# A graph convolution with a residual layer norm: VectorE multiplies both halves of a chunk's vector products in one operation and the selections of two chunks in one operation

## The chip, the cores and the metric

One Trainium2 chip, one of its cores. The time is device microseconds (us) of one execution of the whole program, and the number to predict is the median of a few executions. A few of the profile's times are in nanoseconds (ns) and say so.

## What is computed

12,500 nodes have 128 features each, 32 scalars and 32 vectors of three components. 412,500 edges, sorted by destination, carry four attributes (one scalar, one vector) and eight radial numbers. For each edge the features of its source are gathered, weighted by a small network of the radial numbers and by the attributes, and summed at the destination:

```
h = gelu(gelu(edge_scalar_attr @ W_mlp1) @ W_mlp2)
w00, w01, w10, w11 = h @ Wp_00, h @ Wp_01, h @ Wp_10, h @ Wp_11
out0_a = w00 * e0 * ea0
out0_b = w11 * sum(e1 * ea1, -1) / sqrt(3)
out1_a = (w01 * e0)[:, :, None] * ea1[:, None, :]
out1_b = w10[:, :, None] * e1 * ea0[:, :, None]
n0, n1 = segment_sum([out0_a, out0_b]), segment_sum([out1_a, out1_b])
x = layernorm(x + mix(self(x), n0 @ W2_0e, n1 @ W2_1o))
```

`e0` and `e1` are the scalar and vector features of the edge's source node. Everything is float32 apart from a few small helpers in bfloat16.

## The kernel before

The engines are named as in the profile: PE (TensorE), DVE (VectorE), ACT (ScalarE), POOL (GpSimd), SP (SyncE, which here issues loads and stores alone). They run written-out instruction streams of their own and meet at semaphores.

**Start and end.** The first 155 us transform the nodes, write a table of features to HBM and turn the indices round; the last 84 us finish the last edges, normalise the rows and store them. Between them stands the loop over the edges, which this study is about.

**Blocks, chunks, tiles.** The edges go in 202 blocks of 2048. A block has four chunks (0 to 3) of four tiles, a tile is 128 edges, one per partition. What one block needs, engine by engine:

- POOL gathers the source rows of each tile by an indirect DMA whose indices lie in SBUF (`gather`, L456): 16 a block, 4 a chunk. The gathered rows have four slots, so POOL may run up to four blocks ahead. Before the first gather of block b it waits until chunk 3 of block b-4-1 has been summed by PE and until the indices are there; before chunk c, until DVE has made the products of chunk c of block b-4, which frees the slot.
- PE and ACT make the radial weights (`radial`, L778, out of two layers with a gelu each: PE L764, ACT L551, PE L769, ACT L557). The two layers run several blocks ahead of their use, in halves: each half is a ping-pong of PE, ACT, PE, ACT through one PSUM bank.
- DVE makes for each chunk the products of weights (in PSUM) and gathered rows (in SBUF). `multiply` has one operation for the two scalar parts (L1042, 256 elements a partition) and two for the vector parts (L1045, 384 elements each, half h = 0 and half h = 1). DVE also compares destinations with a window of 32 nodes (`compare`, L1024, once a block) to a 0/1 mask `sel01`, multiplies the mask by the four attributes (`select`, L1032: one operation of 512 elements per chunk, called for two chunks at a time), and adds a finished window into the accumulator (L1073, four a block).
- PE sums the products into the window by matmuls with the selection as weights (`segment_sum`, L790, 32 recorded matmuls a block), transposes the sums (L798) and every fourth block applies the output weights (L805). ACT copies in between (L564 to L566, L570).

**The order on DVE.** One turn (`cycle`) for block b is: products of chunks 2 and 3 of block b, compare for block b+1, products of chunk 0, select for chunks 0 and 1, products of chunk 1, select for chunks 2 and 3, four window additions of an earlier block. Only the last select of a block signals PE (`s_sel`), and each chunk's last product signals for itself (`s_prod`). The products of chunk 2 wait for PE's sum of chunk 2 of the block before (`s_seg`).

**The order on PE.** In a turn it runs second layer, weights of chunk 2, first layer, weights of chunk 3, transposes, second layer, weights of chunks 0 and 1 of a later block, then the 32 matmuls of the segment sums, every fourth turn the output weights, and last a first layer. The body of the hardware loop is eight turns, the loop variable is in the addresses and wait values.

Of the kernel before, what the change touches and what calls it, by code (L numbers as in the profile page):

```python
# [10 lines left out]
ALU = mybir.AluOpType  # L11
# [5 lines left out]
MUL, RADIAL, HID = 32, 8, 64  # L17
# [19 lines left out]
CT = TILES // CHUNKS  # L37
# [7 lines left out]
WINDOW = 32  # L45
# [3 lines left out]
RING = 2 * SUPER  # L49
# [19 lines left out]
def build_program(nc, x, src, dst, ea4, ea8, W1_0e, W1_1o, W_mlp1, W_mlp2, Wp, W2_0e, W2_1o, out):  # L69
# [3 lines left out]
    with ctx:  # L73
        def sb(name, shape, dt=FP32):
            return ctx.enter_context(nc.sbuf_tensor(name, shape, dt))
# [15 lines left out]
        ea_t = sb("ea_t", [128, RING, TILES, 4])  # L91
# [5 lines left out]
        sel = sb("sel", [128, 2, TILES, 4, WINDOW])  # L97
# [44 lines left out]
        sel01 = big.bitcast(BF16)[:, 2 * 12288:2 * 12288 + TILES * WINDOW].rearrange("p (t w) -> p t w", t=TILES)  # L142
# [116 lines left out]
        def nodes_of(j):  # L259
            return 128 if j < NODE_J else REST  # L260
# [25 lines left out]
        for e in range(2):  # L286
            h = slice(HID * e, HID * (e + 1))
# [636 lines left out]
        def _(dve):  # L924
# [37 lines left out]
            for n in range(NODE_BATCHES):  # L962
# [5 lines left out]
                if n < NODE_BATCHES - 1:  # L968
                    last = dve.tensor_copy(feat_rows[:, piece % PIECE_SLOTS, j:j + BATCH, :],
                                           bank[2 + n % 2][:, :].rearrange("p (j f) -> p j f", j=BATCH))  # L970
                else:
                    for i, t in enumerate(batch_tiles(n)):
                        last = dve.tensor_copy(feat_rows[0:nodes_of(t), piece % PIECE_SLOTS, j + i, :],
                                               bank[2 + n % 2][0:nodes_of(t), 128 * i:128 * (i + 1)])
# [52 lines left out]

            def select(b, s, chunks):
                dve.wait_ge(s_sel0, b + 1)
                for c in chunks:  # L1030
                    t = slice(CT * c, CT * (c + 1))
                    last = dve.tensor_tensor(sel[:, s % 2, t], sel01[:, t, :].unsqueeze(2).to_broadcast([128, CT, 4, WINDOW]),  # L1032
                                             ea_t[:, s % RING, t, :].unsqueeze(3).to_broadcast([128, CT, 4, WINDOW]), ALU.mult)
                if CHUNKS - 1 in chunks:
                    last.then_inc(s_sel, 1)

            def multiply(weights, rows, to, n):

                w = weights.rearrange("q (t h a u) -> q t h a u", t=n, h=2, a=2)
                f = rows.rearrange("q t (s u) -> q t s u", s=4)  # L1040
                o = to.rearrange("q t (h s u) -> q t h s u", h=2, s=4)
                dve.tensor_tensor(o[:, :, :, 0, :], w[:, :, :, 0, :],  # L1042
                                  f[:, :, 0, :].unsqueeze(2).to_broadcast([128, n, 2, MUL]), ALU.mult)
                for h in range(2):
                    last = dve.tensor_tensor(o[:, :, h, 1:4, :],  # L1045
                                             w[:, :, h, 1, :].unsqueeze(2).to_broadcast([128, n, 3, MUL]),
                                             f[:, :, 1:4, :], ALU.mult)
                return last

            def products(b, s, c, round_):  # L1050
                dve.wait_ge(s_w[c], b + 1)
                dve.wait_ge(s_g[s % SLOTS][c], round_ * (16 * CT) + 16 * CT)
                if c < 2 and s > 1:
                    dve.wait_ge(s_seg[c], b - 1)
                if c >= 2 and s > 0:
                    dve.wait_ge(s_seg[c], b + 0)
                multiply(wgt_ps[c][:, :], gath[:, s % SLOTS, CT * c:CT * (c + 1), :], prod_at(s, c), CT).then_inc(s_prod[c], 1)
# [17 lines left out]
            def cycle(b, s, n, first_add=2, last=False):  # L1075
                if s >= 0:
                    products(b, s, 2, n * 2 + s // SLOTS)
                    products(b, s, 3, n * 2 + s // SLOTS)
                if s >= -1:
                    compare(b + 1, s + 1, (n + (s + 1) // RING) * 16 + 16)  # L1080
                    if not last:
                        products(b + 1, s + 1, 0, n * 2 + (s + 1) // SLOTS)
                    select(b + 1, s + 1, range(0, 2))
                    if not last:
                        products(b + 1, s + 1, 1, n * 2 + (s + 1) // SLOTS)
                    select(b + 1, s + 1, range(2, CHUNKS))
                    base = load_bases(b - 5) if s >= first_add else None
                if s >= first_add:
                    add_windows(b - 5, s - 5, n * (RING // CONV) + (s - 5) // CONV + 1, base)
# [27 lines left out]
            with dve.If(flag < WINDOW):  # L1117
# [8 lines left out]
                n = ROUNDS - 1  # L1126
# [78 lines left out]
```

## Time and profile before

| | |
|---|---|
| times of three executions | 5050.67, 5320.28, 5044.24 us |
| median | 5050.67 us |
| span of the profiled execution | 5064.0 us |
| busy in it: PE, POOL, DVE, ACT | 3676, 3174, 1878, 1336 us |
| granted TensorE clock, mean | 0.853 |

The profiled execution is one more run, 13.3 us over the median. Its page gives busy time and instructions of each engine, the costliest groups of instructions and the idle time ahead of them with what ended it. "remote" there means that the semaphore update that ended the wait could not be put down to an instruction's recorded end. The timeline has one row per instruction, or per run of like instructions: start and duration in us, engine, line, operation, tiles, count, and in brackets the idle time of the engine ahead of it. The tile names `big` and `dst_rows` stand for reused memory: as an output of L1042 and L1045 they are the products, as an output of L1024 and an input of L1032 the mask.

### The profile page before, as it was taken

The page shows a single profiled execution, that of the slowest core. Times are in us where ns is not written, and L with a number is a line of the kernel's source. Part 1 is how long each engine was busy: PE and PEld are TensorE (multiplying, and loading weights), DVE is VectorE, ACT ScalarE, POOL GpSimd, SP SyncE. Part 2 cuts the span into 40 slices and gives each one's busy share as a digit, 9 for nine tenths or more (in the row PEclk, how much of TensorE's full clock was granted, in tenths as well). Part 3 has the DMA queues.
Part 4 walks back from the last instruction along what each step waited for, and adds up shares of the span by engine and source line. Part 5 has one row for each costly group of instructions (what it writes and reads, how often), then busy time and mean ns, then how long its engine had stood idle before and what let it go on. Part 6 is the DMA issues. An engine that isn't in the chain of part 4 may idle for free.

```text
span 5064.0 us, 44347 instructions
## 1 busy us (share of the span) xinstructions
PE 3676.4 (73%) x13222; PEld 2593.1 (51%) x13222; DVE 1877.7 (37%) x4551; ACT 1336.2 (26%) x2651; POOL 3173.6 (63%) x3262
## 2 busy tenths in 40 slices
PE   7667777777777776667787777677677777777776
PEld 4445455545555544445555555455455545555555
DVE  4333333333334333333433333333333334333335
ACT  4222222222222222222222222222222222222224
POOL 5556666666666665556666666666666666666660
PEclk8788888888888887888888888888888888888887
DMA  4111211211211111111112111111111111111111
GB/s 160 46 43 48 50 46 48 50 46 48 50 47 48 50 46 44 41 44 47 47 48 50 46 48 50 46 48 50 46 46 48 49 47 47 50 48 46 48 45 57
DMA packets 244371, 254.65 MB, mean 50 GB/s; under 512 B 162332, under 2 KB 188703, under 8 KB 242800
## 3 DMA queue, kind: packets, MB, share of 16 engines
q0 software_dynamic: 103616, 211.52, 16.0%
q1 hardware_dynamic: 139024, 42.54, 3.4%
q10 hardware_dynamic: 1696, 0.18, 0.0%
q8 instruction: 15, 0.25, 0.0%
q14 instruction: 20, 0.16, 0.0%
HBM read 241.18 MB, written 12.80 MB: 50 GB/s over the span
## 4 chain that ended last, share of the span: by engine, by line
another core or an unknown queue 57%; PE 28%; ACT 8%; issue 6%; DVE 1%; ACTq 0%; DVEq 0%; POOL 0%; POOLq 0%
PE bank L778 9%; PE bank L769 9%; PE bank L764 6%; ACT h L551 3%; PE bank L790 2%; PE bank L798 1%; ACT big L557 1%; ACT idx L536 1%; ACT ztsb L570 1%; ACT big L622 1%; ACT dst_rows L566 1%; ACT dst_rows L565 1%; ACT dst_rows L564 0%; PE bank L710 0%
## 5 line engine op out<-in xcount | busy, mean ns | idle before, releaser
L456 POOL DMA_INDIRECT gath<-feature_table,idx x3224 | 3151.4, 977 | 1765.7 <-issue 1632.3
L769 PE MATMUL bank<-h,w2bd 128*128 128x512 f32 x800 | 590.7, 829 | 1249.3 <-ACT h L551 1154.6
L1042 DVE TENSOR_TENSOR big<-bank,gath 128x256 f32<-128x256 f32 x606 | 254.9, 421 | 2952.3 <-remote 2656.2
L551 ACT ACTIVATE h<-bank 128x512 f32<-128x512 f32 x400 | 238.9, 597 | 3320.3 <-remote 2863.0
L790 PE MATMUL bank<-big,sel 128*128 128x256 f32 x4848 | 1084.1, 380 | 11.2 <-DVE big L1045 7.3
L778 PEld LDWEIGHTS bank<-wpbd,big 128*128 128x128 f32 x3224 | 747.7, 232 | 524.3 <-issue 364.2
L790 PEld LDWEIGHTS bank<-big,sel 128*128 128x128 f32 x4848 | 924.2, 191 | 138.3 <-issue 7.5
L778 PE MATMUL bank<-wpbd,big 128*128 128x256 f32 x3224 | 971.1, 442 | 1.2 <-DVE big L1045 1.2
L769 PEld LDWEIGHTS bank<-h,w2bd 128*128 128x128 f32 x800 | 153.5, 240 | 1421.3 <-ACT h L551 1317.4
L1045 DVE TENSOR_TENSOR big<-bank,gath 128x384 f32<-128x384 f32 x1212 | 614.0, 549 | 0.0
L1032 DVE TENSOR_TENSOR sel<-big,ea_t 128x512 f32<-128x512 bf16 x808 | 527.9, 695 | 0.0
L557 ACT ACTIVATE big<-bank 128x512 f32<-128x512 f32 x400 | 437.6, 1094 | 93.3 <-PE bank L769 35.0
L790 PE MATMUL bank<-dst_rows,sel 128*128 128x256 f32 x1600 | 361.6, 379 | 0.0
L790 PEld LDWEIGHTS bank<-dst_rows,sel 128*128 128x128 f32 x1600 | 303.9, 190 | 41.3
L764 PE MATMUL bank<-e8T,w1bd 128*128 128x512 f32 x400 | 261.0, 738 | 28.2 <-ACT big L557 19.7
L764 PE MATMUL bank<-dst_rows,w1bd 128*128 128x512 f32 x400 | 256.3, 728 | 30.6 <-ACT big L557 29.2
L1045 DVE TENSOR_TENSOR dst_rows<-bank,gath 128x384 f32<-128x384 f32 x400 | 202.8, 550 | 0.0
L1073 DVE TENSOR_TENSOR acc<-acc,bank 128x32 f32 x806 | 149.8, 186 | 140.6 <-remote 39.1
L805 PE MATMUL bank<-ztsb,dst_rows 128*128 128x512 f32 (+1 forms) x408 | 183.4, 593 | 0.7 <-ACT ztsb L570 0.7
L570 ACT COPY ztsb<-bank 128x512 f32<-128x512 f32 x202 | 118.3, 586 | 180.8 <-PE bank L798 89.8
L564 ACT COPY dst_rows<-bank 32x256 f32<-32x256 f32 x403 | 142.6, 354 | 35.8 <-PE bank L790 31.0
L566 ACT COPY dst_rows<-bank 64x256 f32<-64x256 f32 x403 | 147.9, 367 | 4.8
(90 smaller groups left out, 1426.5 us busy)
## 6 DMA issues: line engine op xcount, KB each, us to landing
gath<-feature_table,idx POOLq DMA_INDIRECT x3224
e<-in_edge_attr SPq DMA_DIRECT2D x204, 64.0 KB
ea_t<-in_edge_attr SPq DMA_DIRECT2D x100, 64.0 KB
feature_table<-gath SPq DMA_DIRECT2D x4, 1280.0 KB, 5.7
out<-big SPq DMA_DIRECT2D x4, 1280.0 KB
big<-in_x SPq DMA_DIRECT2D x3, 1280.0 KB, 10.1
dst_rows<-in_dst SPq DMA_DIRECT2D x1, 1536.0 KB
big<-in_src SPq DMA_DIRECT2D x1, 1280.0 KB
```

The costliest lines, as they stand in the source:

```text
L456: pool.indirect_dma_start(out=gath[:, s % SLOTS, t, :], out_offset=None, in_=table[:, :], in_offset=bass.IndirectOffsetOnAxis(ap=idx[:, s, ...
L551: act.activation(h1[:, h, :], hid_ps[:, :], ACT.Gelu_apprx_tanh, scale=1.0 / math.sqrt(RADIAL)).then_inc(s_h1[h], 1)
L557: act.activation(h2_columns(k // SUPER % 2, 2 * m + h), hid_ps[:, :].rearrange("q (b c p) -> q b c p", b=SUPER, c=CHUNKS), ACT.Gelu_apprx_ ...
L566: act.copy(to[64:128], z_ps[pair][64:128, :, 128:256]).then_inc(s_zc, 1)
L764: pe.matmul(hid_ps[:, :], w1bd[:, 2 * (k % SUPER) + h, :], e8T[k // SUPER % 2][:, :], start=True, stop=True)\
L769: pe.matmul(hid_ps[:, :], w2bd[:, :], h1[:, h, :], start=True, stop=True).then_inc(s_h2p[h], 1)
L778: last = pe.matmul(wgt_ps[c][:, 256 * r:256 * (r + 1)], h2[:, s // SUPER % 2, s % SUPER, c, r, :, :].rearrange("q p l -> q (p l)"), wpbd[: ...
L790: last = pe.matmul(z_ps[c // 2][:, c % 2, :], sel[:, s % 2, CT * c + t, :, :].rearrange("q k w -> q (k w)"), prod_at(s, c)[:, t, :], start ...
L805: last = pe.matmul(y_ps[:, 0:128 * n], conv[:, k, :], ztsb[:, k, 0:n, :, :].rearrange("q b c w -> q (b c w)"), start=(k == 0), stop=(k == 3))
L1032: last = dve.tensor_tensor(sel[:, s % 2, t], sel01[:, t, :].unsqueeze(2).to_broadcast([128, CT, 4, WINDOW]), ea_t[:, s % RING, t, :].unsqu ...
L1042: dve.tensor_tensor(o[:, :, :, 0, :], w[:, :, :, 0, :], f[:, :, 0, :].unsqueeze(2).to_broadcast([128, n, 2, MUL]), ALU.mult)
L1045: last = dve.tensor_tensor(o[:, :, h, 1:4, :], w[:, :, h, 1, :].unsqueeze(2).to_broadcast([128, n, 3, MUL]), f[:, :, 1:4, :], ALU.mult)
```

## The change

Two helpers of DVE are written with wider access patterns. The loop over the halves in `multiply` goes: one operation with 768 elements a partition takes the place of two with 384. The loop over chunks in `select` goes: one operation with 1024 elements takes the place of two with 512. All waits and signals stay at the same places, and so do the orders of the other engines.

```
             def select(b, s, chunks):
                 dve.wait_ge(s_sel0, b + 1)
-                for c in chunks:
-                    t = slice(CT * c, CT * (c + 1))
-                    last = dve.tensor_tensor(sel[:, s % 2, t], sel01[:, t, :].unsqueeze(2).to_broadcast([128, CT, 4, WINDOW]),
-                                             ea_t[:, s % RING, t, :].unsqueeze(3).to_broadcast([128, CT, 4, WINDOW]), ALU.mult)
+                t, n = slice(CT * chunks[0], CT * (chunks[-1] + 1)), CT * len(chunks)
+                last = dve.tensor_tensor(sel[:, s % 2, t], sel01[:, t, :].unsqueeze(2).to_broadcast([128, n, 4, WINDOW]),
+                                         ea_t[:, s % RING, t, :].unsqueeze(3).to_broadcast([128, n, 4, WINDOW]), ALU.mult)
                 if CHUNKS - 1 in chunks:
                     last.then_inc(s_sel, 1)
...
                 dve.tensor_tensor(o[:, :, :, 0, :], w[:, :, :, 0, :],
                                   f[:, :, 0, :].unsqueeze(2).to_broadcast([128, n, 2, MUL]), ALU.mult)
-                for h in range(2):
-                    last = dve.tensor_tensor(o[:, :, h, 1:4, :],
-                                             w[:, :, h, 1, :].unsqueeze(2).to_broadcast([128, n, 3, MUL]),
-                                             f[:, :, 1:4, :], ALU.mult)
-                return last
+                return dve.tensor_tensor(o[:, :, :, 1:4, :],
+                                         w[:, :, :, 1, :].unsqueeze(3).to_broadcast([128, n, 2, 3, MUL]),
+                                         f[:, :, 1:4, :].unsqueeze(2).to_broadcast([128, n, 2, 3, MUL]), ALU.mult)
```

On DVE, the second turn of the opening (the turns written out ahead of the hardware loop) before the change, from the products of chunk 2 to the scalar product of chunk 1; in brackets stand the semaphores waited for, and `x2` is two instructions:

```order
L1042 TENSOR_TENSOR big<-bank,gath 128x8x32 [waits segments_summed2,gathered1_2,radial_weights_done2]
L1045 TENSOR_TENSOR big<-bank,gath 128x4x96 x2
L1042 TENSOR_TENSOR big<-bank,gath 128x8x32 [waits segments_summed3,gathered1_3,radial_weights_done3]
L1045 TENSOR_TENSOR big<-bank,gath 128x4x96 x2
L1024 TENSOR_TENSOR big<-rel_all,iota_w 128x512 [waits selection_ready,segments_summed3,attributes_in3]
L1042 TENSOR_TENSOR big<-bank,gath 128x8x32 [waits segments_summed0,gathered2_0,radial_weights_done0]
L1045 TENSOR_TENSOR big<-bank,gath 128x4x96 x2
L1032 TENSOR_TENSOR sel<-big,ea_t 128x512 [waits onehot_ready]
L1032 TENSOR_TENSOR sel<-big,ea_t 128x512
L1042 TENSOR_TENSOR big<-bank,gath 128x8x32 [waits segments_summed1,gathered2_1,radial_weights_done1]
```

and the same stretch of the changed kernel, whose lines have moved up by one to three:

```order
L1041 TENSOR_TENSOR big<-bank,gath 128x8x32 [waits segments_summed2,gathered1_2,radial_weights_done2]
L1043 TENSOR_TENSOR big<-bank,gath 128x8x96
L1041 TENSOR_TENSOR big<-bank,gath 128x8x32 [waits segments_summed3,gathered1_3,radial_weights_done3]
L1043 TENSOR_TENSOR big<-bank,gath 128x8x96
L1024 TENSOR_TENSOR big<-rel_all,iota_w 128x512 [waits selection_ready,segments_summed3,attributes_in3]
L1041 TENSOR_TENSOR big<-bank,gath 128x8x32 [waits segments_summed0,gathered2_0,radial_weights_done0]
L1043 TENSOR_TENSOR big<-bank,gath 128x8x96
L1031 TENSOR_TENSOR sel<-big,ea_t 128x1024 [waits onehot_ready]
L1041 TENSOR_TENSOR big<-bank,gath 128x8x32 [waits segments_summed1,gathered2_1,radial_weights_done1]
```

Each pair has become one instruction, with the same neighbours: per block four L1045 pairs and two L1032 pairs, twelve instructions, are now six. PE, ACT, SP and POOL have the rows they had.

## Rows read from the trace of the kernel before

**Rows 1.** The page: busy time, and four of its costliest groups.
```profile
PE 3676.4 (73%) x13222; PEld 2593.1 (51%) x13222; DVE 1877.7 (37%) x4551; ACT 1336.2 (26%) x2651; POOL 3173.6 (63%) x3262
...
L456 POOL DMA_INDIRECT gath<-feature_table,idx x3224 | 3151.4, 977 | 1765.7 <-issue 1632.3
L1042 DVE TENSOR_TENSOR big<-bank,gath 128x256 f32<-128x256 f32 x606 | 254.9, 421 | 2952.3 <-remote 2656.2
...
L1045 DVE TENSOR_TENSOR big<-bank,gath 128x384 f32<-128x384 f32 x1212 | 614.0, 549 | 0.0
L1032 DVE TENSOR_TENSOR sel<-big,ea_t 128x512 f32<-128x512 bf16 x808 | 527.9, 695 | 0.0
```

**Rows 2.** Busy us (and instructions) of PE, PEld, DVE, ACT, POOL; clock: seven turns.
```profile
2428.23:2595.58 167.35, 130.22 (x444) 90.61 (x444) 61.98 (x148) 43.36 (x86) 109.03 (x112) 0.83 0.19 49
```

**Rows 3.** Timeline, DVE, one turn and the start of the next two.
```profile
2452.11 0.42 DVE L1042 TENSOR_TENSOR big<-bank,gath 128x256 f32<-128x256 f32 x1 [14.62 <-remote]
2452.45 1.01 DVE L1045 TENSOR_TENSOR big<-bank,gath 128x384 f32<-128x384 f32 x2
2453.38 0.41 DVE L1042 TENSOR_TENSOR big<-bank,gath 128x256 f32<-128x256 f32 x1
...
2454.64 0.68 DVE L1024 TENSOR_TENSOR big<-rel_all,iota_w 128x512 bf16<-128x512 bf16 x1
...
2456.50 1.29 DVE L1032 TENSOR_TENSOR sel<-big,ea_t 128x512 f32<-128x512 bf16 x2
2457.70 0.42 DVE L1042 TENSOR_TENSOR big<-bank,gath 128x256 f32<-128x256 f32 x1
...
2458.97 1.33 DVE L1032 TENSOR_TENSOR sel<-big,ea_t 128x512 f32<-128x512 bf16 x2
...
2476.04 0.42 DVE L1042 TENSOR_TENSOR big<-bank,gath 128x256 f32<-128x256 f32 x1 [14.68 <-remote]
...
2500.37 0.42 DVE L1042 TENSOR_TENSOR big<-bank,gath 128x256 f32<-128x256 f32 x1 [15.08 <-remote]
```

**Rows 4.** Timeline, POOL, the same turn.
```profile
2453.00 0.95 POOL L456 DMA_INDIRECT gath<-feature_table,idx  x1 [3.75 <-issue]
...
2456.77 1.25 POOL L456 DMA_INDIRECT gath<-feature_table,idx  x1 [0.30 <-issue]
...
2459.58 0.96 POOL L456 DMA_INDIRECT gath<-feature_table,idx  x1 [0.30 <-issue]
...
2472.16 0.95 POOL L456 DMA_INDIRECT gath<-feature_table,idx  x1 [0.30 <-issue]
```

**Rows 5.** Timeline, PE: the last matmuls of that turn.
```profile
2469.80 1.02 PE L764 MATMUL bank<-e8T,w1bd 128*128 128x512 f32 x2
```

**Rows 6.** Timeline, POOL and then DVE: the next turn, one of the kind in which gather 2 starts late.
```profile
2476.92 0.95 POOL L456 DMA_INDIRECT gath<-feature_table,idx  x1 [3.81 <-issue]
2478.79 1.28 POOL L456 DMA_INDIRECT gath<-feature_table,idx  x1 [0.92 <-issue]
...
2501.20 0.96 POOL L456 DMA_INDIRECT gath<-feature_table,idx  x1 [3.49 <-issue]
...
2478.57 0.68 DVE L1024 TENSOR_TENSOR big<-rel_all,iota_w 128x512 bf16<-128x512 bf16 x1
...
2480.43 1.28 DVE L1032 TENSOR_TENSOR sel<-big,ea_t 128x512 f32<-128x512 bf16 x2
```

**Rows 7.** Timeline, DVE and POOL: a gather that begins inside the second select.
```profile
2018.71 1.29 DVE L1032 TENSOR_TENSOR sel<-big,ea_t 128x512 f32<-128x512 bf16 x2
...
2019.33 1.50 POOL L456 DMA_INDIRECT gath<-feature_table,idx  x1 [0.30 <-issue]
```

**Rows 8.** The gathers' own line: count, durations in ns (lowest/median/highest).
```profile
L456 POOL DMA_INDIRECT gath<-feature_table,idx x3224: 949/955/1500, 56.1 to 4952.0; - x190
```

**Rows 9.** Timeline, ACT and POOL: one of the long stops.
```profile
2058.12 0.60 ACT L551 ACTIVATE h<-bank 128x512 f32<-128x512 f32 x1 [36.42 <-remote]
...
2075.87 0.95 POOL L456 DMA_INDIRECT gath<-feature_table,idx  x1 [21.87 <-issue]
```

## The prediction

> **What bounds the kernel now.** I read the page first. DVE, the one engine that the change touches, is busy for 1878 of 5064 us, POOL for 3174, PE for 3676 [rows 1]. So no engine looks full, and the waits have to tell. DVE's idle time stands almost whole in front of the first product of chunk 2, 2952 us, of which 2656 are "remote" [rows 1]: an update arrives that fits no instruction's recorded end.
>
> The timeline of one turn shows what is strange about it. DVE starts chunk 2 at 2452.11, works for 9 us and sits idle until 2476.04 [rows 3]. That product waits for PE's sums. PE's matmuls of the turn, the sums among them, are recorded as ended at 2469.80 + 1.02 = 2470.82 [rows 5], 5.2 us before DVE goes on. So neither DVE's nor PE's work sets the end of the turn.
>
> POOL fits. It starts the 16 gathers 0.89 us after DVE's chunk 2 (2453.00 against 2452.11), ends the last at 2472.16 + 0.95 = 2473.11, and 2.93 us later DVE is released [rows 3, 4]. In the next turn the last gather ends at 2501.20 - 3.49 = 2497.71, DVE follows at 2500.37, 2.66 us later, and POOL at 2501.20, 0.83 us after that [rows 3, 6]. A turn is thus 20.1 us of gathers and 3.6 to 3.8 us between the last gather and the next first one. Seven turns took 167.35 us, 23.91 each [rows 2]. I read this as a loop of two: PE's updates reach the waiting engines only when POOL pauses, and POOL goes on only after such an update. Why the update is late the trace does not say; that it follows the last gather does show. POOL's time per turn is then the kernel's time per turn, 201 times over, and all of DVE's work is beside it.
>
> **How DVE still reaches POOL.** A gather takes 0.955 us and starts 1.26 us after the one before (10 gathers from 2459.58 to 2472.16); the longest took 1.50 [rows 4, 8]. The stretched ones lie beside DVE's operations with both inputs in SBUF. Gather 4 of the turn starts at 2456.77, inside the first operation of a select pair, which runs from 2456.50 for 0.69 us (695 ns mean on the page) to 2457.19; the gather ends at 2458.02, 0.83 us after it [rows 1, 3, 4]. A gather begun at 2478.79 beside the compare of 2478.57 to 2479.25 ends at 2480.07, 0.82 after [rows 6]. The one at 2019.33 meets the second operation of a pair, whose end is 2018.71 + 1.29 = 2020.00, and ends at 2020.83, again 0.83 after [rows 7]. So a gather needs something 0.12 us after its start (0.955 - 0.83) and gets it only when the DVE operation that holds it has ended. The products, with one input in PSUM, do not do this.
>
> The Trainium skill, "SBUF — State Buffer", section "Who interferes with whom", has the rule: a VectorE instruction with two SBUF inputs and a GpSimd instruction that reads SBUF exclude each other, whoever starts first, for the whole instruction. The three rows agree for operations of 512 elements. The rule speaks against this change, since it would hold for 1024 elements too; if instead the lock were given back halfway, the sum below would be near nothing.
>
> Who wins when both start together can be read as well. The gather at 2459.58 begins 0.01 us after the second operation of the last pair (2458.97 + 0.60); it keeps its 0.96, and the pair takes 1.33 in place of 1.29, so DVE waited [rows 3, 4]. The gather of rows 7 begins 0.02 us after its operation (2019.33 against 2019.31) and loses 0.54. The edge lies between, at under 20 ns.
>
> **The change part by part.**
> - *Products: four pairs a turn become four operations.* A pair of 384 elements takes 0.93 us to the next start, 0.465 each, and 256 elements take 0.34 [rows 3]; select's 512 take 0.60 (2457.70 - 2456.50 = 1.20 for two). That is about 1.04 ns an element and 0.065 us per operation besides. A merged product takes 0.865 and saves 0.065. At worst the wider pattern saves nothing; the nearest rows give no reason for that, so I take 0.065. These products hold nothing of POOL's, and in themselves are worth zero, hidden by the 14.68 us that DVE idles in a turn [rows 3].
> - *Selects: two pairs become two operations.* 0.69 + 512 x 1.04 ns = 1.22 us long, next start after 1.135. Saved again 0.065 each, again hidden. All in all DVE is done 0.39 us earlier in a turn, if the cover were gone worth 201 x 0.39 = 78 us.
> - *The longer lock, ordinary turn.* Three merged products lie ahead of the first select, so it starts at 2456.50 - 0.195 = 2456.31 and ends at 2457.53. Gather 4 still starts at 2456.77 and now ends at 2457.53 + 0.83 = 2458.36 instead of 2458.02: +0.34 us. The start of POOL moves by 0.06 between turns (0.83 to 0.89), the gather stays inside the operation, and the difference stays 0.34.
> - *The turn in which a gather starts late* (0.92 idle ahead of it in place of 0.30 [rows 6]); I count one in seven, 29. Compare comes 0.13 earlier, so the gather at 2478.79 ends at 2479.95, 0.12 sooner. The next at 2480.25 meets the first select's start (2480.43 - 0.195 = 2480.235); suppose it wins. The one after is clear, the one at 2482.77 falls into the second select, 2480.235 + 2.335 = 2482.57 to 2483.79, with 0.05 of DVE's own wait 2483.84, and ends at 2484.67 instead of 2483.72. Together -0.12 + 0.95 = +0.83 us.
> - *The race.* In the ordinary turn the next gather starts at 2458.36 + 0.30 = 2458.66 and the second select at 2458.97 - 5 x 0.065 = 2458.645: 0.015 us apart, the same race as before, by my arithmetic 2 ns nearer to losing. It now costs 1.22 + 0.83 - 0.955 - 0.015 = 1.08 when lost, where it cost 0.54. How often it is lost now: gathers took 3151.4 us, 72.5 over 3224 x 0.955 [rows 1, 8]; the seven turns have 109.03 - 112 x 0.955 = 2.07 over, 0.30 a turn [rows 2], 59 in 201 turns; the 13 left are some 24 lost races at most, one in ten. I take 15% after: 201 x 0.15 x 1.08 = 33, less 13 that go: +20. The ends are no loss at all (-13) and all lost (201 x 1.08 - 13 = +204).
>
> **The sum.** 172 x 0.34 = 58, 29 x 0.83 = 24, races +20: POOL's time grows by 102 us. How much arrives? The long turn of rows 6 has 20.79 us of gathers against 20.11 and took 24.33 against 23.93: 0.40 of 0.68. Over many turns POOL's time has nowhere to hide; bounds 0.6 and 1, I take 0.95: +97. On the profiled execution, 5064.0 to 5161; that one lies 13.3 us over the median of 5050.67, so I forecast 5148 us, 1.9% slower. For the lock the ends are: given back after 512 elements, and all held. In the first case earlier selects even shorten the stretch by up to 0.195 us a turn, -39; in the second, with every race lost, +82 + 204 = +286.
>
> **The rivals.**
> 1. *Most races are lost.* Only a few ns decide, and the merged operations shift the meeting. For: the lost one of rows 7 stands 10 ns from the won one of rows 3 and 4. Against: my sum moves the meeting by 2 ns only. Half lost: 201 x 0.5 x 1.08 - 13 + 82 = 178, 5229 us; all lost, 5337. Chance 0.2, middle 5250.
> 2. *The lock is not longer, or POOL is not the bound*: no change, 5015 to 5065, say 5045. For: no row shows an operation of 1024 elements, and PE's release is explained by nothing in the trace. Against: rows 3, 4 and 6. Chance 0.2.
> 3. *Faster: DVE's earlier products and selects shorten the turn.* Place: the products of chunk 2 feed the weights on PE. It decides if the release of DVE depends on DVE's own earlier work, at a price of up to 0.39 us a turn, 78 us, 4973 us. Against: DVE idles 14.7 us a turn, PE is done 5.2 us early. The Trainium skill, "VectorE: DVE Perf Modes", section "Rules for kernel authors", advises to reduce the number of operations because each pays its fixed time; the 0.065 us agree, but this time lies under a wait. Chance 0.05.
> 4. *The rhythm of POOL and PE's late updates breaks more often.* Some stops are long: ACT waits 36.42 us, POOL stops for 21.87 instead of 3.7 [rows 9], 18 us lost each. One of the three executions before took 5320.28, as if 15 such came. Ten more than now: about 5148 + 180 = 5330. Chance 0.08.
>
> **How the numbers follow.** My forecast has 0.47, with 5148 and its own range 5110 to 5190. The range reaches down through rival 2 and up through the half of rival 1: 5030 to 5290, which leaves out about 0.05 below and 0.12 above. Two per cent, about what a measurement of this kernel can tell from no change, are 101 us: 5152. Slower by more: 0.45 of my forecast's 0.47, or 0.21, rival 1 with 0.19, rival 4 with 0.08, together 0.48. Within 2%: the other 0.26, rival 2 with 0.19, rival 3 with 0.03: 0.48. Faster: 0.04.
>
> **What would show it.** If right, the merged select takes 1.22 us and the fourth gather of an ordinary turn about 1.63 in place of 1.25; POOL's mean per gather rises from 977 to about 1009 ns (102 us over 3224); the turn grows from 23.9 to 24.4; gathers that lose take about 2.03 us, a length that no gather has today; DVE's busy time falls, and its idle time grows by more. Wrong on the lock: no gather over 1.5 us. Wrong on the bound: longer gathers and the same turn. Wrong on the race: many gathers of 2.03 us.

## The result, and the profile after

The changed kernel took 5207.53 us in the median of four runs (5133.43, 5205.85, 5209.4, 5209.22). The kernel before took 5067.01 in the median of four (5050.67, 5320.28, 5044.24, 5083.34), one of them run beside the new ones. The ratio is 1.0269; ratios here and below leave out runs over 1.5% above the fastest of the same kernel (here 5320.28, in the third set 5443.69 and 5378.69). Its 95% interval is 1.0165 to 1.0373. So the change makes this kernel slower; the interval leaves open whether it is by over 2%. The profiled execution of the changed kernel is the shortest, 5133.43 us; the other three have no trace.

The page of the changed kernel, the lines that answer to [rows 1]:

```profile
span 5131.6 us, 43137 instructions
...
PE 3740.6 (73%) x13222; PEld 2607.6 (51%) x13222; DVE 1809.0 (35%) x3341; ACT 1333.5 (26%) x2651; POOL 3254.0 (63%) x3262
...
L456 POOL DMA_INDIRECT gath<-feature_table,idx x3224 | 3231.8, 1002 | 1738.9 <-issue 1649.2
...
L1041 DVE TENSOR_TENSOR big<-bank,gath 128x256 f32<-128x256 f32 x606 | 255.3, 421 | 3086.3 <-remote 2278.9
...
L1043 DVE TENSOR_TENSOR big<-bank,gath 128x768 f32<-128x768 f32 x606 | 574.4, 948 | 0.0
L1031 DVE TENSOR_TENSOR sel<-big,ea_t 128x1024 f32<-128x1024 bf16 x404 | 502.0, 1243 | 0.0
```

DVE has 69 us less to do and idles longer in front of chunk 2. POOL's gathers, whose code is untouched, take 80.4 us more in all (3231.8 against 3151.4), a mean of 1002 ns against 977. The span grew by 67.6; 14.3 of it lie behind the last gather, where the kernel before has 111.0 us and the changed one 125.3.

An ordinary turn of the changed kernel, POOL's timeline (start, duration, and the idle time ahead in brackets) and then DVE's, to be laid beside [rows 3, 4]:

```profile
2545.20 0.95 POOL L456 DMA_INDIRECT gath<-feature_table,idx  x1 [3.96 <-issue]
...
2548.97 1.64 POOL L456 DMA_INDIRECT gath<-feature_table,idx  x1 [0.30 <-issue]
2550.92 0.96 POOL L456 DMA_INDIRECT gath<-feature_table,idx  x1 [0.30 <-issue]
...
2564.77 0.95 POOL L456 DMA_INDIRECT gath<-feature_table,idx  x1 [0.30 <-issue]
2569.08 0.95 POOL L456 DMA_INDIRECT gath<-feature_table,idx  x1 [3.36 <-issue]
```

```profile
2544.37 0.42 DVE L1041 TENSOR_TENSOR big<-bank,gath 128x256 f32<-128x256 f32 x1 [16.89 <-remote]
2544.71 0.95 DVE L1043 TENSOR_TENSOR big<-bank,gath 128x768 f32<-128x768 f32 x1
...
2548.57 1.22 DVE L1031 TENSOR_TENSOR sel<-big,ea_t 128x1024 f32<-128x1024 bf16 x1
...
2550.90 1.27 DVE L1031 TENSOR_TENSOR sel<-big,ea_t 128x1024 f32<-128x1024 bf16 x1
...
2568.16 0.42 DVE L1041 TENSOR_TENSOR big<-bank,gath 128x256 f32<-128x256 f32 x1 [14.91 <-remote]
```

The fourth gather begins inside the first merged select, which ends at 2548.57 + 1.22 = 2549.79, and ends itself at 2550.61, 0.82 later: the hold is as long as the operation. The gather at 2550.92 begins 0.02 after the start of the second select, keeps its 0.96, and the select takes 1.27. But the turn is 2569.08 - 2545.20 = 23.88 us, no longer than the 23.92 from 2453.00 to 2476.92 in [rows 4, 6]: POOL's pause shrank from 3.81 to 3.36 and swallowed the 0.39 by which the fourth gather grew (1.64 against 1.25). These are single turns; means follow in the third set.

### The profile page after: what moved, and what is told of

Its sections match the earlier page's. It is cut to its first block, busy times and chain, and to the rows that moved or that the text cites. A ratio compares the mean times of both kernels' runs of the same rounds, so it can differ in the third digit from the quotient of the medians.

```text
span 5131.6 us, 43137 instructions
## 1 busy us (share of the span) xinstructions
PE 3740.6 (73%) x13222; PEld 2607.6 (51%) x13222; DVE 1809.0 (35%) x3341; ACT 1333.5 (26%) x2651; POOL 3254.0 (63%) x3262
## 4 chain that ended last, share of the span: by engine, by line
PE 41%; another core or an unknown queue 39%; issue 11%; ACT 7%; DVE 1%; ACTq 0%; DMA 0%; DVEq 0%; POOL 0%; POOLq 0%
PE bank L778 11%; PE bank L790 10%; PE bank L769 9%; PE bank L764 6%; PE bank L805 2%; ACT h L551 2%; PE bank L798 2%; ACT big L557 1%; ACT dst_rows L566 1%; ACT dst_rows L565 1%; ACT big L622 1%; ACT idx L536 1%; ACT dst_rows L564 1%; PE bank L723 0%
## 5 line engine op out<-in xcount | busy, mean ns | idle before, releaser
L456 POOL DMA_INDIRECT gath<-feature_table,idx x3224 | 3231.8, 1002 | 1738.9 <-issue 1649.2
L790 PE MATMUL bank<-big,sel 128*128 128x256 f32 x4848 | 1111.8, 384 | 66.3 <-issue 56.3
L1043 DVE TENSOR_TENSOR big<-bank,gath 128x768 f32<-128x768 f32 x606 | 574.4, 948 | 0.0
L1031 DVE TENSOR_TENSOR sel<-big,ea_t 128x1024 f32<-128x1024 bf16 x404 | 502.0, 1243 | 0.0
L764 PE MATMUL bank<-dst_rows,w1bd 128*128 128x512 f32 x400 | 260.4, 738 | 53.3 <-ACT big L557 32.7
L764 PE MATMUL bank<-e8T,w1bd 128*128 128x512 f32 x400 | 257.3, 730 | 46.5 <-ACT big L557 23.4
L805 PE MATMUL bank<-ztsb,dst_rows 128*128 128x512 f32 (+1 forms) x408 | 201.6, 631 | 16.6 <-issue 15.5
L1043 DVE TENSOR_TENSOR dst_rows<-bank,gath 128x768 f32<-128x768 f32 x200 | 189.5, 948 | 0.0
```

The costliest lines, as they stand in the source:

```text
L456: pool.indirect_dma_start(out=gath[:, s % SLOTS, t, :], out_offset=None, in_=table[:, :], in_offset=bass.IndirectOffsetOnAxis(ap=idx[:, s, ...
L764: pe.matmul(hid_ps[:, :], w1bd[:, 2 * (k % SUPER) + h, :], e8T[k // SUPER % 2][:, :], start=True, stop=True)\
L790: last = pe.matmul(z_ps[c // 2][:, c % 2, :], sel[:, s % 2, CT * c + t, :, :].rearrange("q k w -> q (k w)"), prod_at(s, c)[:, t, :], start ...
L805: last = pe.matmul(y_ps[:, 0:128 * n], conv[:, k, :], ztsb[:, k, 0:n, :, :].rearrange("q b c w -> q (b c w)"), start=(k == 0), stop=(k == 3))
L1043: return dve.tensor_tensor(o[:, :, :, 1:4, :], w[:, :, :, 1, :].unsqueeze(3).to_broadcast([128, n, 2, 3, MUL]), f[:, :, 1:4, :].unsqueeze( ...
```

## The experiments

The chip did not behave the same all day, with the same kernels. In the first and second set and in the last one the kernel before took 4218 us, 17% less than in the runs above; in the third it took 5072, with single runs up to 5444. In the traces of the quick behaviour PE's updates do not come late, and POOL never pauses between blocks. In the changed kernel's quick trace the matmuls of L764 end at 2123.41 and ACT, which waits for them, starts at 2123.45; in [rows 5] they end at 2470.82, and ACT starts at 2476.07. The granted clock of TensorE differs too: 0.937 to 0.965 in the quick runs, 0.839 to 0.864 in the others. PE is busy 3487.8 us in the changed kernel's quick trace and 3740.6 in the slower one, for the same 13222 matmuls. Which of the two brings the other, if either does, no run shows. The kernel before has no trace in the quick behaviour. Ratios are taken only within a set.

In all diffs the lines with - are those of the kernel named.

### First set: each half of the change alone

**The changed kernel again.**

> The changed kernel once more, for a second trace and times beside the kernel before on one chip. Lock theory: mean gather 1000 to 1010 ns against 977 before (75 us more over 3224 gathers), every select 1.22 us or, where the gather came first, 1.27 us; the time 1.5 to 3% over the kernel before. If the time is at the upper end, gathers of about 2.03 us, races lost, should be more than the few of the first trace. Rival (the gathers do not set the turn): the time differs by less than 1%, or it differs by a good deal more than the gathers grow.

4291.82 us against 4218.47, ratio 1.0174 (1.0157 to 1.0191), as expected; the gathers' mean of 987 ns is below the 1000 to 1010 that were expected. The page:

```profile
L456 POOL DMA_INDIRECT gath<-feature_table,idx x3224 | 3181.1, 987 | 1002.7 <-issue 980.9
L1041 DVE TENSOR_TENSOR big<-bank,gath 128x256 f32<-128x256 f32 x606 | 257.4, 425 | 1782.0 <-PE bank L790 1173.8
```

POOL's idle time is 1002.7 us, 0.31 a gather, the fixed distance from one to the next: POOL works without a pause, and a turn is 20.67 us. "remote" is gone from DVE's waits.

**Only the selects merged** (the two products of a chunk as before).

> Only the selections are merged, the vector products stay two operations. Lock theory: the merged select starts 0.195 us later than in the changed kernel, so the fourth gather of a turn is stretched by 0.80 to 0.88 us where it was 0.24 to 0.34 before, and the gather that would race the second select starts 0.05 us ahead of it and is safe. Gathers' stretch in all about 180 us against 75 before: mean gather 1010 ns, time about 105 us over before (2%), like the changed kernel or a little slower. Rival, that the merged products carry the loss: no change against before.

4221.35, ratio 1.0003 (0.9993 to 1.0014). Not slower: the expected 2% fell, and so did the expected stretch of 180 us (35 in the trace).

**Only the products merged** (two selects as before).

> Only the vector products are merged, the selections stay at 512 elements. Lock theory: nothing holds the port longer, but the selections come 0.195 and 0.26 us earlier, which moves them against the gathers: the fourth gather is stretched by 0.10 to 0.16 us (before 0.24 to 0.34), the sixth now starts 0.08 us inside the second half of the second select and loses about 0.48. Stretch in all about 135 us against 75 before: mean gather 997 ns, time about 60 us over before (1.2%). Rival, that only the longer lock costs: time as before or some us faster. Rival, that DVE's own time counts: 52 us faster.

4262.56, ratio 1.01 (1.0083 to 1.0117): 44 us slower from operations that hold nothing, where some 60 were expected.

**Products merged, the selects cut into four** of 256 elements instead of joined to one:

```
-                for c in chunks:
-                    t = slice(CT * c, CT * (c + 1))
+                for at in range(CT * chunks[0], CT * (chunks[-1] + 1), 2):
+                    t = slice(at, at + 2)
```

> The vector products merged, the selections split into operations of 256 elements (two tiles), eight a turn where the kernel before has four. Lock theory: a gather waits at most for an operation of 0.42 us; stretch in all about 45 us against 75 before, mean gather 969 ns, no gather over 1.35 us, time 15 to 30 us under the kernel before though DVE works about as long as in it. Rival, that DVE's operations or their number set the turn: slower than the changed kernel's by up to 6 x 0.065 x 201 = 78 us, and not faster than before.

4257.52, ratio 1.0093 (1.0076 to 1.011). It was expected to be faster than before and was not: 470 gathers were held, more than in any other kernel, by 0.14 us each in the mean. The longest gather took 1.47 us, where at most 1.35 was expected.

The gathers' groups of the three:

```profile
L456 POOL DMA_INDIRECT gath<-feature_table,idx x3224 | 3111.5, 965 | 1002.5 <-issue 981.5
```
```profile
L456 POOL DMA_INDIRECT gath<-feature_table,idx x3224 | 3151.4, 977 | 1002.5 <-issue 981.7
```
```profile
L456 POOL DMA_INDIRECT gath<-feature_table,idx x3224 | 3144.5, 975 | 1002.4 <-issue 982.2
```

Two things follow. First, the profiled executions (4293.1, 4222.7, 4266.2, 4256.9 us) less their time in gathers give 1112.0, 1111.2, 1114.8 and 1112.4: the time is POOL's gathers and a constant. Second, the two halves of the change do not add up (+3, +44, together +73). Counted in the traces, gathers over 1.0 us ("held" from here on) are 59 with only the selects merged, 184 with only the products merged, and 166 with both; over 1.9 us they are 8, none and 46. In these three traces merging the products raises how many gathers are held, merging the selects for how long.

The timeline of the changed kernel in this set shows both (POOL, then DVE):

```profile
2107.56 0.95 POOL L456 DMA_INDIRECT gath<-feature_table,idx  x1 [0.30 <-issue]
2108.82 0.95 POOL L456 DMA_INDIRECT gath<-feature_table,idx  x1 [0.30 <-issue]
...
2123.93 1.48 POOL L456 DMA_INDIRECT gath<-feature_table,idx  x1 [0.30 <-issue]
```

```profile
2107.65 1.21 DVE L1031 TENSOR_TENSOR sel<-big,ea_t 128x1024 f32<-128x1024 bf16 x1
...
2123.03 0.95 DVE L1043 TENSOR_TENSOR big<-bank,gath 128x768 f32<-128x768 f32 x1
2123.89 0.68 DVE L1024 TENSOR_TENSOR big<-rel_all,iota_w 128x512 bf16<-128x512 bf16 x1
```

A select of 1.21 us fits between two gathers whose starts are 1.26 apart, if it starts at the right moment: here it begins 0.09 us after one gather and ends 0.04 after the next, and holds neither. The compare at 2123.89 begins 0.04 before a gather and holds it until 2125.41, 0.84 after its own end. Had its product been two operations, it would by my reckoning have begun some 0.065 later, after the gather. In this behaviour what follows DVE's products often keeps a fixed distance to POOL's gathers: with only the selects merged, 172 of the 202 first selects and 191 of the second begin within 0.2 us after the start of a gather, with both merges 119 and 126. So 65 ns can decide.

### Second set: what else could carry the time

**More work on DVE**, from the kernel before: two maxima over 512 elements in PSUM in each turn, ahead of the window additions.

```
+                for i in range(2):
+                    dve.wait_ge(s_spare[i], b + 1)
+                    dve.tensor_reduce(spare[:, i:i + 1], y_ps[:, :], AXIS_X, ALU.max).then_inc(s_spare[i], 1)
```

> The kernel before with two more DVE operations a turn, a maximum over 512 elements of PSUM each (about 0.68 us, 1.2 us a turn, 240 us in all), put ahead of the window additions. They have one input, in PSUM, and come after the selections. Theory that POOL's gathers set the turn: less than 15 us, the gathers' mean unchanged at 977 ns. Rival, that DVE's time is on the path: 200 us or more slower.

4228.20 against 4217.97, ratio 1.0023 (1.0014 to 1.0033). The group of the added operation, and the gathers' line:

```profile
L1072 DVE TENSOR_REDUCE spare<-bank 128x1 f32<-128x512 f32 x404 | 258.8, 682 | 18.6 <-PE bank L807 17.4 <-issue 1.2
```
```profile
L458 POOL DMA_INDIRECT gath<-feature_table,idx x3224 | 3102.7, 962 | 1002.6 <-issue 981.5
```

259 us of DVE's time cost 10. At least half of the 10 lies behind the last gather: 80.1 us to the end, where the other quick traces have 71.9 to 74.9. DVE is hidden. The added maxima, which read only PSUM, hold no gather by themselves: every gather of the loop that was held ended 0.82 to 0.84 us after a compare or a select, none after a maximum.

**A little work on POOL**, from the kernel before: two memsets of 32 columns ahead of chunk 2's gathers.

```
+                        if c == 2:
+                            for i in range(2):
+                                pool.wait_ge(s_spare[i], b + 1)
+                                pool.sem_inc(s_round, 1)
+                                pool.memset(spare[:, 32 * i:32 * i + 32], 0.0).then_inc(s_spare[i], 1)
```

> The kernel before with two more POOL operations a turn, zeroing 32 columns each, between chunks 1 and 2 of the gathers, in the middle of POOL's stretch. DVE, ACT and PE unchanged. Theory that POOL's gathers set the turn: the turn grows by what the first to last gather of a block grows, d us in the trace, and the time by about 200 x d (expected d 0.4 to 1.2 us, so 80 to 240 us). Rival, that the stretched gathers are hidden and the loss comes from elsewhere: the time does not change.

4240.01, ratio 1.0054 (1.0037 to 1.007).

```profile
2106.10 0.95 POOL L458 DMA_INDIRECT gath<-feature_table,idx  x1 [0.30 <-issue]
2107.06 0.20 POOL L486 MEMSET spare<- 128x32 f32 x2
2107.41 0.96 POOL L458 DMA_INDIRECT gath<-feature_table,idx  x1 [0.16 <-issue]
```

The memsets lie in the distance between two gathers and make it 0.05 us longer (1.31 for 1.26), 10 us over 202 blocks. That is far less than the 0.4 to 1.2 us a turn that were expected, and the time is 22 us over before instead of 80 to 240. The rest is in the gathers: 3121.1 us, of which 44.7 are stretch (the sum of what each takes over 0.955). The profiled 4245.1 less 3121.1 less the 10 is 1114, the constant of the first set. So POOL's time arrives in full; how much stretch the kernel before has in this behaviour was not traced.

### Third set: with PE's late updates

**The kernel before, with a profile.**

> The kernel before with a trace on the chips of the experiments, where it takes 4218 us and not 5050. The four kernels traced so far lie on one line, time = 1110 us + time in gathers (3181.1 and 4291.8; 3111.5 and 4221.4; 3151.4 and 4262.6; 3144.5 and 4257.5). Theory that POOL's gathers set the turn: 4218 - 1110 = 3108 us in gathers, a mean of 964 ns. Rival: a mean of 977 ns as in the first trace, and the time then has another cause.

5412.01 us for the profiled run; the seven of the set are 5443.69, 5378.69, 5052.69, 5072.31, 5104.27, 5068.57 and 5056.96. This answers nothing of what was expected, since the quick behaviour was gone. The kernel before has two rhythms of its own here: with the four runs of the result's section, eight of its twelve executions took 5044 to 5104 us and four 5320 to 5444.

**Both merges, and a maximum over two elements of PSUM ahead of each merged product**, which puts the 65 ns back:

```
                 if c is not None:
+                    dve.tensor_reduce(spare[:, c:c + 1], weights[:, 0:2], AXIS_X, ALU.max).then_inc(s_spare[c], 1)
```

> The changed kernel with one tiny DVE operation (a maximum over two PSUM elements, about 65 ns to the next start) ahead of each merged product. All selections and comparisons thus start when they would in the kernel with only the selections merged, while both merges stay. Theory that the position against the gathers decides: mean gather about 965 ns in place of 987, time about 4222 us in place of 4292, faster by 70 us though DVE does more. Rival, that the merged operations cost by themselves: 4292 us or more.

5363.53, ratio 1.059 (1.0522 to 1.0658). In this trace 138 gathers take 1.9 us or more, 8 in the changed kernel's. The ratio is against the quicker rhythm of the kernel before. All four runs of this kernel, 5353 to 5400, lie where four of the kernel before's twelve lie too, so how much of the 5.9% its operations cost is not shown.

**The second select moved ahead of chunk 1's products**, from the changed kernel:

```
                     select(b + 1, s + 1, range(0, 2))
+                    select(b + 1, s + 1, range(2, CHUNKS))
...
-                    select(b + 1, s + 1, range(2, CHUNKS))
```

> The changed kernel with the second select ahead of the products of chunk 1, so that two selects of 1.22 us stand back to back; the control for psum_select. Lock theory: a stretch of 2.3 us in which a gather gets in once, so mean gather 985 to 1030 ns and a time on the line 1110 us + gathers, 4285 to 4430 us. Rival: as the changed kernel, 4292 us.

5249.78, ratio 1.0357 (1.0287 to 1.0426).

**The same order, and the selects read PSUM instead of the mask.** This kernel leaves the mask out of all selections but the last block's; radial weights stand in its place, so its sums are others.

```
+                dve.wait_ge(s_w[1], b + 1)
+                mask = wgt_ps[1][:, 0:n * WINDOW].rearrange("q (t w) -> q t w", t=n)
-                last = dve.tensor_tensor(sel[:, s % 2, t], sel01[:, t, :].unsqueeze(2).to_broadcast([128, n, 4, WINDOW]),
+                last = dve.tensor_tensor(sel[:, s % 2, t], mask.unsqueeze(2).to_broadcast([128, n, 4, WINDOW]),
```

> As order_only, but the select multiplies the attributes by the radial weights of chunk 1, which lie in PSUM, in place of the mask in SBUF (the last block's select keeps the mask): as many elements and operations, one input in SBUF instead of two. The edges are no longer put where they belong; the mask is left out of the sums. Lock theory: no gather is stretched beside a select, only beside a compare, so mean gather 955 to 962 ns and a time of 4190 to 4212 us, under the kernel before. Rival, that the length of DVE's operations disturbs POOL whatever they read: as order_only.

4964.85, ratio 0.9789 (0.9741 to 0.9838), 285 us less than the kernel with the second select moved. The two differ by the operand, which is also float32 instead of bfloat16, and by a wait for the radial weights, which costs DVE nothing in this trace (0.0 us idle before the 402 selects). The gathers' groups and own lines (there in ns, lowest/median/highest), first of the kernel that reads the mask, then of the one that reads PSUM:

```profile
L456 POOL DMA_INDIRECT gath<-feature_table,idx x3224 | 3230.4, 1002 | 1839.8 <-issue 1737.5
...
L456 POOL DMA_INDIRECT gath<-feature_table,idx x3224: 949/955/1968, 55.9 to 5104.9; - x190
```
```profile
L456 POOL DMA_INDIRECT gath<-feature_table,idx x3224 | 3084.4, 957 | 1729.0 <-issue 1600.8
...
L456 POOL DMA_INDIRECT gath<-feature_table,idx x3224: 949/955/1327, 55.2 to 4847.4; - x190
```

and the timeline of the second, DVE and then POOL:

```profile
2519.56 2.35 DVE L1033 TENSOR_TENSOR sel<-bank,ea_t 128x1024 f32<-128x1024 f32 x2
```
```profile
2518.71 0.95 POOL L456 DMA_INDIRECT gath<-feature_table,idx  x1 [0.30 <-issue]
2519.97 0.96 POOL L456 DMA_INDIRECT gath<-feature_table,idx  x1 [0.30 <-issue]
2521.23 0.95 POOL L456 DMA_INDIRECT gath<-feature_table,idx  x1 [0.30 <-issue]
```

Gathers begin in the middle of selects as long as before (1215 ns in the mean, 1220 in the other) and are not held. Counting only those that begin at least 0.035 us after the start of a select and at least 0.13 before its end, it is none of 366 here and all 199 there. The 30 gathers held in this loop all lie beside the compare, which still has both inputs in SBUF. The products are float32 with one input in PSUM: in the changed kernel 478 gathers begin inside them, and none is held. This shows the cause of the stretch: not the length of a DVE operation by itself, but its inputs, and with the compare and the products beside it the reading is two inputs in SBUF. An operation with two float32 inputs in SBUF does not occur beside the gathers, so place and type are not wholly taken apart. The Trainium skill, "SBUF — State Buffer", section "Who interferes with whom", says that a VectorE instruction with two SBUF inputs contends with a GpSimd instruction that reads SBUF; the runs agree, with stretches of 155 us for the one and 9 us for the other.

**What the late updates do to it.** I call a turn ordinary if POOL's pause ahead of the next block is 3 to 5 us. From the starts and ends of the gathers in the traces (199 turns each; held: over 1.0 us; the stretch is the sum over 0.955):

| kernel | held | stretch us | ordinary turns | their mean us | span us |
|---|---|---|---|---|---|
| select reads PSUM | 33 | 8.7 | 192 | 23.69 | 4959.2 |
| before, first profile | 216 | 75.6 | 180 | 23.88 | 5064.0 |
| changed | 226 | 155.9 | 121 | 24.06 | 5131.6 |
| second select earlier | 226 | 155.0 | 89 | 23.95 | 5229.6 |
| merged, with tiny maxima | 229 | 191.3 | 67 | 24.10 | 5371.5 |
| before, this set's profile | 283 | 129.2 | 48 | 23.85 | 5410.1 |

The ordinary turn hardly grows: 0.18 us from before to changed, where its gathers grew by 0.31. The span follows the number of ordinary turns. The other 78 of the changed kernel have pauses of 0.30 us (26), 1 to 3 us (27), 5 to 8 (6) and 8 to 18 (19), such as this one:

```profile
2838.69 0.95 POOL L456 DMA_INDIRECT gath<-feature_table,idx  x1 [13.84 <-issue]
```

Six traces in the same order by span and by ordinary turns show that the two belong together. The first and fourth rows, which differ by the select's operand, show that held gathers have a part in it: without them there are 192 ordinary turns instead of 89, and the 285 us are about twice the 146 of stretch that went. The stretch alone does not set the rhythm: the last kernel has less of it than the third.

### Last set: position or merge

The kernel with the tiny maxima and the one with only the selects merged should have selects and compares at the same distance from the products ahead of them; only the one has the products merged. In this set the chip was in its quick behaviour. Two executions of it, one of the kernel with the maxima (11792.4 us) and one of the kernel before (13790.0), had a granted clock of 1.0 and no trace; they stay unexplained.

> The kernel of the run pad once more, now beside sel_only on one chip. In both, comparisons and selections start at the same distance from the products of chunk 2, and one has the vector products merged, the other not. Theory that only the position against the gathers decides: the two agree within 15 us (0.3%), wherever they land: both at about 4222 us and 36 us of stretch where the kernel before takes 4218, or both at about 5360 us where it takes 5070. Rival, that the merged products or the additional operation cost by themselves: pad_2 is slower than sel_only by 70 us or more.

4214.37 against 4218.09, ratio 0.9992 (0.9982 to 1.0002).

> The kernel of the run sel_only once more, beside pad_2. Where the kernel before takes 4218 us: 4221 us again. Where it takes 5070: by the theory of position as pad, 5340 to 5390 us, with 190 us of stretch in the gathers and more long stops; by the rival (the merged selects are harmless, as they were on the other occasion) 5070 us.

4227.21, ratio 1.0014 (1.0001 to 1.0027). The gathers' groups, with the maxima and with only the selects merged:

```profile
L458 POOL DMA_INDIRECT gath<-feature_table,idx x3224 | 3099.7, 961 | 1002.6 <-issue 981.8
```
```profile
L456 POOL DMA_INDIRECT gath<-feature_table,idx x3224 | 3113.9, 966 | 1002.6 <-issue 981.2
```

They are 13 us apart, 0.3%, within the 15 that were expected. The changed kernel took 4291.82 in the first set, 1.74% over the kernel before; with four operations more in each turn it takes 77 us less and is level with it (0.9992), and 42 gathers are held for 166. So there it is the moment at which the selects and the compare begin that costs, not the merge.

## Why the prediction was right, and where it was not

The measured 5207.53 lies in the stated range, 60 us over the predicted 5148. The mechanism is the predicted one in what it does to the gathers; the sum is not, and the hit owes much to the width of the range, which reaches up for rival 1.

- *POOL's time is the kernel's time.* Right. Without late updates each profiled run is its gathers and 1111 to 1115 us, but for the two with added work (1119.8 with the maxima on DVE, 1124.0 with the memsets); 259 us more on DVE cost 10. With late updates it is right only loosely, as below.
- *The lock holds for the whole merged operation.* Right: 1.64 us was measured for the fourth gather where "about 1.63" was predicted, the end 0.82 us after the select's where 0.83 was taken. In all 14 traces 2394 gathers begun inside a select or compare were held, and every one ends 0.82 to 0.84 us after it. The operand swap shows the cause.
- *Merged product 0.065 less, merged select 1.22 us, both hidden.* Right in duration. Wrong in "in themselves are worth zero": the products' 65 ns are hidden, but they move what follows, and without late updates that costs 44 us by itself. With late updates the sum did take in this shift for the first select (2456.31), and there it held.
- *The stretch, 58 + 24 + 20 = 102 us.* It was 80.4. What was mis-sized lies at the second select: its late turns (29 x 0.95 = 28) and races (+20) make 47 us of the sum. The trace has 24 gathers held by it, 22.4 us in all (8 of them of 1.9 us or more), where the kernel before has 16 and 8.7: +14. The first select and the compare gave more than was put down for them, +66 where the sum has 55 (58 less 29 x 0.12). The edge is about where it was put: the gather of 2550.92, 0.02 us after the select, won. By the rounded rows the gather starts 0.015 us after the select instead of 0.010, 5 ns nearer to losing and not 2; rows of 0.01 us can't tell the two apart.
- *"I take 0.95: +97".* This step failed. The prediction passed on 0.95 of POOL's added time. The ordinary turn gave 0.18 for 0.31, a share of 0.6, which was the lower bound; the row of the long turn (0.40 of 0.68) had said it, and the prediction argued it away. 121 such turns are 22 us. The 199 turns of the profiled run take 199 x (24.62 - 24.33) = 58 us more than before, so 36 come from the turns that are not ordinary, 78 in place of 19: rival 4, which had a chance of 0.08, in small. That the profiled run lies 67.6 us over the one before, and not far from the 97, is luck: two errors that partly cancel. The three untraced runs lie some 75 us above the profiled one, so the median is 157 over the forecast's starting point of 5050.67. No trace says what those 75 are; races lost as in rival 1 (5229 for half of them) or a broken rhythm as in rival 4 would both fit.
- *Rival 1* (most races lost) fell in the profiled execution of the changed kernel, though the kernel with tiny maxima is near it: 138 gathers of 1.9 us or more, and 5363.53 us. *Rival 2* fell with the fourth gather. *Rival 3* (faster) fell: idle time took DVE's gain.

**Open.** What makes PE's updates late, and only on some occasions with the same kernel: no run here changes it. Whether the three untraced runs near 5207 have some 100 ordinary turns, as the table would suggest, was not seen. Whether the lower granted clock is a cause of the late updates or follows from them, no run tells. Held gathers have a part in breaking the rhythm, but what else does was not tried by itself: the kernel before has both rhythms with no edit at all. A kernel of this form that computes the reference and is faster than before was not found: the one with the tiny maxima is within 0.2% of it without late updates and lies at 5353 to 5400 us with them.

## What to carry to other kernels

Ask of a merge not only what it saves on its engine, but whom it holds up for longer and what it moves. Here a VectorE operation with two SBUF inputs beside GpSimd's indirect DMAs costs nothing if it fits between two of the moments, some 0.12 us after a gather's start, at which the gathers can be held. An estimate from the rows: of the 1.26 us between gathers, an operation of 1.22 us can begin in only some 0.18 without holding one (from 0.015 before to 0.165 after a gather's start), one of 0.69 in some 0.71. If the engine that gains is idle anyway, the merge has nothing to win. What helped here was one input in PSUM; where the operations began mattered as much as their length.

## What was not expected

- An indirect gather of 0.955 us that begins inside an operation with two SBUF inputs ends 0.82 to 0.84 us after it, up to 2.02 us long; if it begins up to 0.035 us after the operation's recorded start it can win, and DVE waits some 0.05. Between 0.011 and 0.035 both outcomes occur in the traces.
- Two inputs in SBUF are not the only thing that holds a gather. A cast of L993 (int32 to float32, 512 elements, from SBUF to SBUF, one input) does it too, ahead of the loop: with only the selects merged, the gather at 83.82 takes 1.09 us and ends 0.83 after the cast of 83.67 to 84.08.
- The same kernel on the same chip took 4218 us and later 5072, and in the second case between 5053 and 5444. The traces differ by late updates of PE, POOL's pauses and a lower granted clock. In the changed kernel, traced in both, the gathers differ by 51 us (3231.8 against 3181.1) of the 840 between the spans.
- Four added operations a turn made the changed kernel 77 us faster where nothing came late.
